# Key projection in three products of split parts, with new tables and every period written out

## The reference

```python
x = layernorm(x + attn(x, wq, wk, wv))                   # softmax over the queries, then triu
q = (x @ Wq + bq), k = (context @ Wk + bk), v = (context @ Wv + bv)   # 16 heads of 8 channels
a = softmax(clip(q k^T * 8**-0.5, -10000, 10000))        # per batch and head: 56 x 1500
x = layernorm(x + (a v) @ Wo + bo)
probs = softmax(x @ Wr); top 2 of 8 experts, at most cap tokens each
x = layernorm(x + sum_e gate_e * (relu(x @ W1[e]) @ W2[e]))
```

## Time and profile before

| | us |
|---|---|
| median of three runs | 942.42 |
| the profiled execution | 942.79 |
| its span | 941.1 |
| TensorE busy | 894.5 |
| VectorE busy | 718.5 |
| ScalarE busy | 629.3 |
| GpSimd busy | 366.0 |
| mean granted TensorE clock | 0.984 |

### The profile page before, as it was taken

How to read it: one execution, slowest core, us unless ns; L and a number is a source line. 1 busy time by engine, 2 the same in 40 slices (tenths; PEclk the granted TensorE clock), 3 DMA queues, 4 the chain that set the end, 5 groups by cost and what they waited for, 6 DMA issues and landing times.

```text
span 941.1 us, 28147 instructions
## 1 busy us (share of the span) xinstructions
PE 894.5 (95%) x10439; PEld 736.6 (78%) x10439; DVE 718.5 (76%) x1481; ACT 629.3 (67%) x1081; POOL 366.0 (39%) x351
## 2 busy tenths in 40 slices
PE   5789999999999997999999999999999899999995
PEld 4657787878888875877878888877887778999894
DVE  6667787777777774777777777777777767777997
ACT  3666777777777775777777777777775544545554
POOL 6553443333333332333333333333355431113992
PEclk8999999999999998999999999999999999999998
DMA  6559666655566666366655566666646001002331
GB/s 146 115 117 210 143 145 145 148 128 124 125 141 155 146 146 135 83 145 146 147 129 125 125 141 153 147 144 141 144 101 145 25 7 40 23 23 103 118 118 43
DMA packets 36547, 112.55 MB, mean 120 GB/s; under 512 B 8322, under 2 KB 18884, under 8 KB 36292
## 3 DMA queue, kind: packets, MB, share of 16 engines
q1 hardware_dynamic: 36404, 110.64, 51.8%
HBM read 32.23 MB, written 1.89 MB: 36 GB/s over the span
## 4 chain that ended last, share of the span: by engine, by line
PE 90%; DVE 5%; ACT 2%; issue 2%; POOL 0%; ACTq 0%; DVEq 0%
PE psum L1448 18%; PE psum L1633 18%; PE psum L1694 13%; PE psum L1455 9%; PE psum L1460 8%; PE psum L1698 4%; PE psum L1721 3%; PE psum L1722 3%; PE psum L1734 3%; PE psum L1723 3%; PE psum L1733 3%; PE psum L1735 3%; DVE arena L967 1%; DVE arena L906 1%; PE psum L1766 0%
## 5 line engine op out<-in xcount | busy, mean ns | idle before, releaser
L967 DVE TENSOR_REDUCE arena<-psum 128x1 f32<-128x500 f32 x672 | 435.7, 674 | 156.3 <-PE psum L1448 151.3
L778 ACT ACTIVATE arena<-psum 125x896 f32<-125x896 f32 x384 | 334.5, 916 | 127.1 <-PE psum L1633 66.7
L1448 PE MATMUL psum<-K_hi,Q_bd 128*128 128x500 f32 x672 | 286.8, 465 | 9.1 <-DVE arena L967 2.9
L552 POOL TENSOR_TENSOR arena<-arena,K_hi 128x500 fp32r<-128x500 f32 x96 | 119.8, 1248 | 382.8 <-ACT K_hi L710 382.8
L1633 PEld LDWEIGHTS psum<-Q_st,K_st 103*125 103x125 f32 x1536 | 211.0, 189 | 20.0 <-issue 6.7
L1633 PE MATMUL psum<-Q_st,K_st 103*125 103x224 f32 x1536 | 215.9, 274 | 6.0 <-issue 4.0
L1448 PEld LDWEIGHTS psum<-K_hi,Q_bd 128*128 128x128 f32 x672 | 123.2, 190 | 57.3 <-DVE arena L967 38.9
L1694 PE MATMUL psum<-arena 125*25 125x168 f32 x3072 | 159.5, 310 | 0.7 <-issue 0.6
L834 ACT ACTIVATE K_st<-psum 128x448 fp32r<-128x448 f32 x128 | 69.8, 545 | 79.4 <-PE psum L1723 77.9
L1698 PE MATMUL psum<-arena 125*9 125x56 f32 x3072 | 109.3, 214 | 0.0
L1455 PEld LDWEIGHTS psum<-WvA,arena 97*125 97x125 f32 x768 | 101.3, 191 | 4.1
(11 more groups left out here) (258 smaller groups left out, 1022.7 us busy)
## 6 DMA issues: line engine op xcount, KB each, us to landing
K_st<-K_hi SPq DMA_DIRECT2D x256, 187.5 KB, 4.9
K_st<-arena SPq DMA_DIRECT2D x128, 187.5 KB, 3.4
arena<-in_ctx SPq DMA_DIRECT2D x32, 562.5 KB, 7.2
arena<-gate_rows SPq DMA_DIRECT2D x8, 896.0 KB, 4.3
arena<-in_L_ffn_W SPq DMA_DIRECT2D x16, 256.0 KB, 3.2
arena<-OS_all SPq DMA_DIRECT2D x12, 168.0 KB, 6.9
x_rows<-x_all SPq DMA_DIRECT2D x1, 896.0 KB, 10.0
out<-x_all SPq DMA_DIRECT2D x4, 224.0 KB, 2.5
```

The costliest lines, as they stand in the source:

```text
L552: g.tensor_tensor(low.bitcast(F32R), low, K_hi[:, par, n * KB:n * KB + KB].bitcast(F32), ALU.subtract).then_inc(F["keys_low"], 1)
L778: a.activation(P2[c % NP].rearrange("p (n k) -> p n k", n=2), psum[0:CK, 2 + 2 * (c % 2):4 + 2 * (c % 2), 0:HQ // 2], ACT.Exp)\
L967: v.reduce_max(mx[:, par, n // NB, n % NB:n % NB + 1], bank_of(n)[:, 0:KB], AX.X).then_inc(F["piece_max_taken"], 1)
L1448: mm(bank_of(n)[:, 0:KB], Q_bd[:, par].rearrange("p h q -> p (h q)")[:, 128 * (n // NB):128 * (n // NB) + 128], K_hi[:, par, (n % NB) * KB ...
```

## The change

- The key projections of batches 2 to 31 no longer multiply fp32 operands. `Wk_split` holds the high and low part of the weights; for each 500 keys GpSimd makes the high and low part of the context (`split_context`: a multiplication by ones, then a subtraction) into `ctx_split`, which has one buffer. TensorE makes three fp32r products (high x high, high x low, low x high) into the same bank. Batches 0 and 1 are projected as before.
- GpSimd's period is in a new order, which stands in full in the diff.
- The tables of slots are new: key projections in slots 1, 4, 7 (before 3, 5, 7), values in 8, 11, 3 (before 9, 11, 1), key copies in 1, 5, 7, output chunks in four groups, at slots 3, 6, 9, 11, instead of three.
- `periods` writes out all 33 calls; there is no loop.
- The four weights of the first stage, a product of two of them and its two masks move into memory that the fourth buffer of `P2` takes later.

SyncE's and ScalarE's periods are as before, but for the slots.

```diff
-V_SLOTS = (9, 11, 1)
-K_SLOTS = (3, 5, 7)
-COPY_SLOT, SUM_SLOTS, SCALE_SLOT = 0, (0, 3, 3, 3), 5
-ROW_SLOT, TURN_SLOT, KEEP_SLOT = 7, 8, 10
-V_COPIES = (9, 11, 1)
-K_COPIES = (3, 5, 7)
-NEXT, BEFORE_TURN = 9, 2
-EARLY_PIECES = {1: (9, 10), 2: (12,), 3: (13,), 5: (16,), 7: (19,), 9: (2,), 10: (4,), 11: (5,)}
-MID_PIECES = {1: (11,), 3: (14,), 7: (20, 0), 9: (3,), 11: (6, 7)}
-LATE_PIECES = {3: (15,), 5: (17, 18), 7: (1,), 11: (8,)}
+V_SLOTS = (8, 11, 3)
+K_SLOTS = (1, 4, 7)
+COPY_SLOT, SUM_SLOTS, SCALE_SLOT = 0, (2, 3, 3, 3), 5
+ROW_SLOT, TURN_SLOT, KEEP_SLOT = 7, 8, 11
+V_COPIES = (9, 11, 2)
+K_COPIES = (1, 5, 7)
+NEXT, BEFORE_TURN = 10, 2
+EARLY_PIECES = {1: (10,), 2: (12,), 3: (13,), 4: (15,), 7: (20,), 8: (1,), 11: (5,)}
+MID_PIECES = {4: (16,), 6: (18,), 9: (2,), 10: (4,), 11: (6, 7)}
+LATE_PIECES = {1: (11,), 3: (14,), 5: (17,), 6: (19,), 7: (0,), 9: (3,), 11: (8, 9)}
...
-OUTPUTS = {5: ((0, 0), (0, 1), (0, 2), (0, 3)), 7: ((0, 4), (0, 5), (0, 6), (0, 7)), 11: ((0, 8), (0, 9), (0, 10), (0, 11))}
+OUTPUTS = {3: ((0, 0), (0, 1)), 6: ((0, 2), (0, 3), (0, 4), (0, 5)), 9: ((0, 6), (0, 7), (0, 8)), 11: ((0, 9), (0, 10), (0, 11))}
...
+        ctx_split = sb("ctx_split", [128, 2, KB], F32R)
+        Wk_split = sb("Wk_split", [DC + 1, 2, 128], F32R)
...
-            for b in range(2):
-                period(b, b, 0)
-            with eng.Fori(0, 2) as i:
-                for j in range(2, 14):
-                    period(i * 12 + j, j % 2, i * 6 + j // 2)
-            for b in range(B - 6, B + 1):
+            for b in range(B + 1):
                 period(b, b % 2, b // 2)
...
+            def split_context(b, par, n, load):
+
+                if load:
+                    pool.wait_ge(D_[f"c{par}"], 16 * load)
+                pool.wait_ge(F["keys_made"], b * NB + n + PRIME)
+                part = ctxT2[:, par, n * KB:n * KB + KB]
+                high, low = ctx_split[0:DC + 1, 0], ctx_split[0:DC + 1, 1]
+                step(g.tensor_tensor(high, part, ones[0:DC + 1, 0:1].to_broadcast([DC + 1, KB]), ALU.mult))
+                g.tensor_tensor(low, part, high.bitcast(F32), ALU.subtract).then_inc(F["context_split"], 1)
+
...
+            pool.wait_ge(D_["keyw"], 16 * 2)
+            step(g.tensor_tensor(Wk_split[:, 0], WkA[:], ones[0:DC + 1], ALU.mult))
+            step(g.tensor_tensor(Wk_split[:, 1], WkA[:], Wk_split[:, 0].bitcast(F32), ALU.subtract))
+            pool.wait_ge(S1["queries_made"], NQ)
+            split_context(2, 0, 0, 2)
 
             def period(b, par, half):
                 if has(b, 2):
                     pool.wait_ge(F["max_scores_made"], (b + 1) * PIECES + PRIME)
                     spread_queries(b + 2, par)
+                if has(b, 2):
+                    split_context(b + 2, par, 1, 0)
+                if has(b, 2):
+                    split_context(b + 2, par, 2, 0)
+                if has(b, 2):
+                    low_keys(b + 2, par, (2,))
+                if has(b, 3):
+                    split_context(b + 3, 1 - par, 0, half + 2 + par)
                 if has(b, 1):
                     if not isinstance(b, int) or b >= 1:
                         pool.wait_ge(F["scores_made"], b * NC + PRIME)
...
                     stack_queries(b + 1, 1 - par)
                 if has(b, 2):
-                    low_keys(b + 2, par)
+                    low_keys(b + 2, par, (0,))
+                if has(b, 2):
+                    low_keys(b + 2, par, (1,))
...
+            def key_project_split(b, par, n):
+
+                pe.wait_ge(F["context_split"], b * NB + (n + 1) + PRIME)
+                for i, (w, x) in enumerate(((0, 0), (0, 1), (1, 0))):
+                    last = mm(bank[7][:, 0:KB], Wk_split[:, w], ctx_split[0:DC + 1, x], start=(i == 0), stop=(i == 2))
+                last.then_inc(F["keys_made"], 1)
+
...
                     if c in K_SLOTS and has(b, 2):
                         n = K_SLOTS.index(c)
-                        if n == 0:
-                            pe.wait_ge(D_[f"c{par}"], (half + 2) * 16)
                         bank_free(b, "keys", n)
-                        key_project(par, n, bank[7])
+                        key_project_split(b, par, n)
```

More of the change, by code:

```diff
@@ L116, in decoder_kernel @@
         perm = sb("perm", [128, SLOTS, 128])
-        w_sb = {n: sb(n + "_sb", [128, 128]) for n in ("wq", "wk", "wv", "xWq", "xWo")}
-        qk = sb("qk", [128, 128])
+        ctx_split = sb("ctx_split", [128, 2, KB], F32R)
+        Wk_split = sb("Wk_split", [DC + 1, 2, 128], F32R)
+        xWo_sb = sb("xWo_sb", [128, 128])
         bq_col = sb("bq_col", [128, 1])
@@ L160, in decoder_kernel @@
         start = used[0]
+        first_place = whole[:, start + NP * HQ - HQ:start + NP * HQ]
+        w_sb = {n: first_place[:, 128 * i:128 * i + 128] for i, n in enumerate(("wq", "wk", "wv", "xWq"))}
+        w_sb["xWo"] = xWo_sb[:]
+        qk = first_place[:, 512:640]
+        other_batch, causal = [first_place[0:TT, 640 + TT * i:640 + TT * i + TT] for i in range(2)]
         def first_buffers(place):
@@ L354, in _ @@
         def _(sp):
-            sp.dma_start(w_sb["wq"][:], wq).then_inc(weights, 16)
-            sp.dma_start(w_sb["wk"][:], wk).then_inc(weights, 16)
+            sp.dma_start(w_sb["wq"], wq).then_inc(weights, 16)
+            sp.dma_start(w_sb["wk"], wk).then_inc(weights, 16)
             for n in range(NQ):
@@ L368, in _ @@
             load_context(0, 0)
-            for t, src in ((w_sb["xWq"][:], xWq), (bq_col[:], xbq.rearrange("(p a) -> p a", a=1)),
-                           (w_sb["xWo"][:], xWo), (WvA[0:DC, :], xWv), (WvA[DC:DC + 1, :], xbv.rearrange("(a p) -> a p", a=1)),
+            for t, src in ((w_sb["xWq"], xWq), (bq_col[:], xbq.rearrange("(p a) -> p a", a=1)),
+                           (w_sb["xWo"], xWo), (WvA[0:DC, :], xWv), (WvA[DC:DC + 1, :], xbv.rearrange("(a p) -> a p", a=1)),
                            (bo_col[:], xbo.rearrange("(p a) -> p a", a=1)), (Wr_sb[:], Wr)):
@@ L958, in _ @@
             dve.wait_ge(w_ps, 1)
-            v.tensor_copy(qk[:], bank[0][:, 0:128]).then_inc(w_ev, 1)
+            v.tensor_copy(qk, bank[0][:, 0:128]).then_inc(w_ev, 1)
             dve.wait_ge(consts, 1)
@@ L1374, in first_u @@
                     pe.wait_ge(S1["u_copied"], n - 1)
-                mm(bank[2 + n % 2][:, 0:QC], qk[:], firsts[n].xT, start=True, stop=True).then_inc(S1["u_made"], 1)
+                mm(bank[2 + n % 2][:, 0:QC], qk, firsts[n].xT, start=True, stop=True).then_inc(S1["u_made"], 1)
             def first_scores(n):
@@ L1390, in first_values @@
                 for t in range(QT):
-                    last = mm(bank[4 + n % 2][0:TT, D * t:D * t + D], firsts[n].xT[:, TT * t:TT * t + TT], w_sb["wv"][:], start=True, stop=True)
+                    last = mm(bank[4 + n % 2][0:TT, D * t:D * t + D], firsts[n].xT[:, TT * t:TT * t + TT], w_sb["wv"], start=True, stop=True)
                 last.then_inc(S1["values_made"], 1)
@@ L1434, in first_query @@
                     pe.wait_ge(S1["queries_copied"], n)
-                mm(bank[6][:, 0:QC], w_sb["xWq"][:], firsts[n].xT, start=True, stop=True).then_inc(S1["queries_made"], 1)
+                mm(bank[6][:, 0:QC], w_sb["xWq"], firsts[n].xT, start=True, stop=True).then_inc(S1["queries_made"], 1)
             def piece(b, par, n, turns):
@@ L1487, in _ @@
             pe.wait_ge(weights, 16 * 3)
-            mm(bank[0][:, 0:128], w_sb["wq"][:], w_sb["wk"][:], start=True, stop=True).then_inc(w_ps, 1)
+            mm(bank[0][:, 0:128], w_sb["wq"], w_sb["wk"], start=True, stop=True).then_inc(w_ps, 1)
             pe.wait_ge(w_ev, 1)
@@ L1559, in output_weights @@
                 for s in range(SLOTS - 1):
-                    mm(bank[6][:, 0:128], perm[:, s, :], w_sb["xWo"][:], start=(s == 0), stop=(s == SLOTS - 2))
-                mm(bank[6][:, 128:256], perm[:, SLOTS - 1, :], w_sb["xWo"][:], start=True, stop=True)
+                    mm(bank[6][:, 0:128], perm[:, s, :], w_sb["xWo"], start=(s == 0), stop=(s == SLOTS - 2))
+                mm(bank[6][:, 128:256], perm[:, SLOTS - 1, :], w_sb["xWo"], start=True, stop=True)
                 for s in range(SLOTS - 1):
```

12 lines of the change are left out of this document (5 added, 7 removed).

## The result

The changed kernel takes 1117.9 us (median of four runs, 1114.4 to 1119.1) against 942.6 for the kernel before (median of four as well): a ratio of 1.185, interval 1.181 to 1.189. The prediction had the direction and the mechanism, but its range ended at 1090. The profiled execution has a span of 1112.7, 171.6 more than before.

The account below looks back on a forecast made before the run. A closed ring through GpSimd's low keys, 23.8 us a period, was to replace TensorE as bound: 942.8 + 69.7 (ring) + 2.3 + 5.3 (early periods) + 34.8 (clock) = 1054.9, forecast 1054.5 us; range 1000 to 1090.

Parts of the forecast that it names:

- the ring: Closed chain low-key transfers, ScalarE's key copy, TensorE, GpSimd, transfers again: 23.8 us a period before clock loss, against TensorE's 20.2.
- the clock's term: Half clock after TensorE's idle 3.6 in each period: 1.2 us lost a period, 0 to 1.7; 34.8 over 29 periods.
- TensorE's own part: TensorE from the value product of slot 3 to the last key product, at full clock: 7.5 us.
- TensorE's period without the ring: TensorE alone, with shorter key products, four output groups and waits of 0.5: 20.2 us a period.
- rival C: GpSimd keeps up and TensorE's 20.2 is the period: 908 us, chance 0.12.
- The two small terms: Late start behind period 0's query transfers, +2.3 us, and GpSimd's later constants in period 1, +5.3 us.
- The 2.3 among them: Split of batch 3 waits for a context loaded behind period 0's twelve query transfers: +2.3 us, 0 to 5.
- Key product: Each key product falls from 0.84 to 0.69 us with three products of 500 columns; 0.45 saved a period.
- The page's formula: Product of N columns takes N/2.4 + 2.5 ns: 0.21 us for 500 columns, 0.63 for three.
- Written out: Writing out the loop removes its edge, entry and exit waits: 11 us go, and straight code costs nothing.
- Second ring: Context transfer, then split of the next batch, stacked queries and low keys on GpSimd: 22.2 us, next to take over.
- Rival B: Ring without clock loss, idle time spread over several waits, clock at 2.4 GHz: 1020 us, chance 0.28.

Follow-up runs that it names:

- the one with filler: Changed kernel plus 26 unused products of 256 columns ahead of the wait of TensorE's third value product; 1053.6 us.
- low keys early: Changed kernel with GpSimd's low keys 0 and 1 moved ahead of the last key copy, behind the splits of parts 1 and 2; 952.3 us, ratio 1.010.
- the tables of before: Changed kernel with the slot tables of the kernel before; split parts, three products and GpSimd's order kept; 986.6 us, ratio 1.046.
- the shorter ring: Changed kernel with GpSimd's stacked queries moved out of the stretch from last key copy to low-key transfers, no extra products; 1017.6 and 1035.9 us.
- the one written out: Kernel before with only its loop written out as separate calls; 934.6 us, ratio 0.992.
- the version with the tables of before and three products: Written-out kernel, old tables, three-product keys, split parts in three rotating halves, low keys between splits, later constants in period 30; 935.3 us, ratio 0.991.

## Why the prediction was right, and where it was wrong

**The chain of the ring: right, link by link.** Medians over 25 periods of the changed kernel, and over 27 of the one with filler, from the same marks as in the prediction:

```
link                                   predicted   changed   with filler
first issue to first key copy           5.7         5.71       5.71
copy to value product                   0.6         0.63       0.63
value product to last key product       7.5 + 1.2  10.76       7.97
to GpSimd's low keys                    2.2         2.26       2.25
GpSimd's five steps                     7.6         7.63       7.63
pick-up by SyncE, waits inside          0.2         0.03       0.03
period                                 25.0        27.2       24.2
```

Five of six links, 16.3 us of them, came out within 0.2. That the wait would stand at the value product of slot 3, that the key copy would wait for the DMA, that SyncE would start with GpSimd's last low keys: all there.

**The step that failed: the clock's term, taken as 1.2 a period with an upper bound of 1.7; it measured 2.8.** The rows that it rested on the earlier trace rows showed two drops, one of 6.8 us after an idle 4.0 and one of 3.4 after shorter waits. The forecast wait, 3.6 (3.1 in the trace), was nearer to the first, and I took the second, for the reason that most of that stretch was busy. The measured drop lasts 6.8 us and begins shortly before TensorE's work comes back (322.88 and 323.21 in the turn shown; 0.1 to 2.3 before, 0.75 in the median), so that most of it is paid: 10.76 - 7.97 = 2.8 a period, 1.6 more than taken. The bound was wrong too, since it was drawn from the shorter row alone; by the row of 6.8 it would have been 3.4, and the range would have reached 1139. Over 29 periods the miss is 46 us; with 2.8 in place of 1.2 the same sum gives 1101. The Trainium skill, "TensorE: Matmul & The Clock Gate", Part 1 (What's actually happening), has the half clock as the default that activity lifts; the trace agrees as far as it goes: 27 drops in the 27 periods between 150 and 880 us, and where the filler kept TensorE busy one in the middle stretch for twenty.

**TensorE's own part was too short by 0.5.** 7.97 at full clock for 7.5 (the terms of that sum make 7.55): the outputs start 1.07 after the value product where I had 0.79 and 0.15 for the hand-over, and the seven pieces take 1.93 with the edges behind outputs, not 1.61. 14 us over 29 periods. The same kind of error stands in TensorE's period without the ring: 20.2 predicted, 20.87 measured with low keys early. It made no difference to the forecast, but rival C's 908 was out of reach; the best that these tables gave is 952.

**The sum.** Predicted for the 29 periods 690.2 + 2.3 + 5.3 + 34.8 = 732.6, measured 794.2. The miss of 61.6 is 46 for the clock and 14 for TensorE's part, and 2 that weren't traced. The two small terms, 7.6 together, are 6.6 in the trace: the first two periods are 29.7 and 31.3 long instead of 27.2. The 2.3 among them had no row; the first period's 2.5 is what the trace has in its place, and what makes it wasn't traced.

**The rest.** Key product 0.68 (predicted 0.69), 0.16 saved each. The page's formula quoted in the prediction (the Trainium skill, "TensorE: Matmul & The Clock Gate", Back-to-back issue gap) is one that the section gives for an isolated product; it would have made 0.63 of the three, and the measurement stays with the row. Written out: -8.6 for -11. Second ring: 22.4 for 22.2, shown only with the tables of before. Rival B (ring without clock, 1020) came with the filler only, and at 1054: by accident that is the forecast's number, from a longer ring and no clock loss. The rows that spoke for B, 1.8 idle of 7.0 with the clock at 1.00, show one wait of 1.84 and not several, half the forecast wait and near the 1.4 to 1.7 that kept the clock about half of the time in the shorter ring; they said nothing of a wait of 3 us.

## What to carry to other kernels

Before an engine with time to spare gets work, find which of its instructions starts a transfer that frees a single buffer; work put between the buffer's last reader and that transfer lengthens every period, however idle the engine is on average. Here two instructions of 1.2 us in the wrong place cost 166 us on top of 952.

An idle stretch of TensorE that comes once a period can have two prices, its own length and the clock behind it. Bound the second by the longest half-clock stretch that the trace shows, placed wholly on busy time.

A shorter matmul saves only where TensorE waits for nothing just behind it; look at who empties the next bank, and at who makes the next operands, before counting it.

## What the runs showed of the hardware that I had not expected

- More work for TensorE made the kernel faster: 26 products of 256 columns in a wait of 3.1 us took 64 us off. Only TensorE's link of the ring changed (10.76 to 7.97), and with it the granted clock (0.88 to 1.00 in the middle stretch).
- The drops and the periods keep step. In the changed kernel the drops start 27.31 us apart from 159 to 866 us, with one step of 23.9 among them; the periods are 27.0 to 27.4 in the first half and 26.8 to 28.0 in the second, with 6.8 us at half clock each, and 25.8 in the two where the drop lasted 3.4. Which of the two sets the other wasn't tested. With the shorter ring, whose own period is 22.6, periods of 22.6, 24.2 and 27.2 stand side by side.
- GpSimd and VectorE got in each other's way. VectorE's scaling of the outputs (two inputs, 128 x 224) takes 0.37 us with GpSimd idle (in the kernel before and in the one written out). In the version with the tables of before and three products it starts 0.54 into a GpSimd subtraction and takes 0.98, ending after that, in nearly every period; the GpSimd subtraction behind it takes 1.41 for 1.26:

```profile
311.93 0.98 DVE L1077 SCALAR_TENSOR_TENSOR OS_all<-arena 128x224 f32<-128x224 f32 x1
```

```profile
311.39 1.27 POOL L546 TENSOR_TENSOR arena<-arena,K_hi 128x500 fp32r<-128x500 f32 x1
312.61 1.41 POOL L570 TENSOR_TENSOR ctx_split<-arena,ctx_split 97x500 fp32r<-97x500 f32 x1
```

The Trainium skill, "SBUF — State Buffer", Who interferes with whom, says that the two share a pair of ports and that the later one is blocked until the first is done; 0.37 behind the 0.73 that the subtraction still had to run would be 1.1, the row has 0.98. The one at 416.75 starts 0.23 into the subtraction and takes 1.28; both end 0.25 after it. The waiting is shown, then, and that 0.25 and not the whole 0.37 comes behind it. It cost nothing here, as VectorE then waited 0.62 for TensorE.
